# Causal attention in 32-row groups and units of four heads, instead of 96-row groups and units of two

## The reference, cut to what matters

```python
scores = jnp.einsum('bhqd,bhkd->bhqk', q, k) / jnp.sqrt(jnp.float32(HD))
causal = jnp.tril(jnp.ones((S, S), dtype=bool))
scores = jnp.where(causal[None, None], scores, jnp.finfo(scores.dtype).min)
attn = jax.nn.softmax(scores, axis=-1)
out = jnp.einsum('bhqk,bhkd->bhqd', attn, v)
out = out.transpose(0, 2, 1, 3).reshape(B, S, NQ * HD)
return out @ w_out
```

## Time and profile before

| | |
|---|---|
| median of three runs | 1374.59 us (1372.58 to 1374.79) |
| profiled execution, from the first to the last instruction (span) | 1397.1 us; what it took in all is not shown |
| TensorE (PE) busy | 1113.2 us, 80% of the span |
| VectorE (DVE) busy | 586.6 us, 42% |
| ScalarE (ACT) busy | 394.9 us, 28% |
| GpSimd (POOL) busy | 85.7 us, 6% |
| mean granted clock of TensorE | 0.871 of 2.4 GHz |

### The profile page before, as it was taken

The page is one execution under the profiler, slowest core; times in us unless marked ns, Lnnn a source line. Parts: engine busy times, 40 slices in busy tenths (PEclk is TensorE's granted clock), DMA queues, the critical chain, the costliest instruction groups (busy, mean ns, idle before and its releaser), DMA issues. The chain is left out here.

```text
span 1397.1 us, 24200 instructions
## 1 busy us (share of the span) xinstructions
PE 1113.2 (80%) x8646; PEld 771.9 (55%) x8647; DVE 586.6 (42%) x1737; ACT 394.9 (28%) x939; POOL 85.7 (6%) x128
## 2 busy tenths in 40 slices
PE   1999999998988889797793299955878978369992
PEld 0676677656565566555472177732645654247771
DVE  5272144224343465567486022215752672512222
ACT  2223312221414444343240133312421431013220
POOL 2000000000000000000000400022000000040003
PEclk9999988599999888898795599986979989579996
DMA  9100000000000000291003211118300000021113
GB/s 245 45 3 3 0 2 3 1 1 2 2 2 2 1 1 1 47 238 55 0 1 71 82 43 49 47 44 200 104 1 0 1 1 1 23 74 46 50 43 99
DMA packets 32137, 57.09 MB, mean 41 GB/s; under 512 B 3558, under 2 KB 28871, under 8 KB 31019
## 3 DMA queue, kind: packets, MB, share of 16 engines
q1 hardware_dynamic: 28856, 48.47, 12.8%
q0 software_dynamic: 3072, 6.30, 1.5%
q10 hardware_dynamic: 114, 1.04, 0.3%
HBM read 41.83 MB, written 13.86 MB: 40 GB/s over the span
## 5 line engine op out<-in xcount | busy, mean ns | idle before, releaser
L1932 PE MATMUL banks<-gu,sxT 96*128 x496 | 178.8, 505 | 0.8 <-ACT sxT L1967 0.4
L215 PE MATMUL banks<-xT,weights 96*96 96x512 f32 (+3 forms) x288 | 149.1, 668 | 1.2 <-ACT xT L616 0.9
L1333 ACT ACTIVATE work<-banks,nmax 128x128 f32<-128x128 f32 (+1 forms) x288 | 105.7, 418 | 108.0 <-DVE nmax L1372 107.7
L1993 DVE TENSOR_TENSOR h<-sg,banks 128x384 f32<-128x384 f32 x62 | 34.4, 555 | 237.7 <-ACT sg L1975 227.3
L1932 PEld LDWEIGHTS banks<-gu,sxT 96*128 96x128 f32 x496 | 93.1, 198 | 54.9 <-issue 8.1
L1372 DVE TENSOR_REDUCE nmax<-banks 128x2 f32<-128x256 f32 (+1 forms) x144 | 80.2, 557 | 64.7 <-PE banks L1277 62.4
L1252 PE MATMUL banks<-K,Q 96*128 96x128 f32 (+1 forms) x384 | 86.1, 351 | 11.1 <-PEq L88 11.1
L215 PEld LDWEIGHTS banks<-xT,weights 96*96 96x96 f32 (+3 forms) x288 | 53.5, 193 | 74.8 <-issue 67.3
L555 PE MATMUL banks<-Q,K 64*98 64x196 f32 (+2 forms) x960 | 78.7, 305 | 9.1 <-ACT work L688 9.1
L688 ACT ACTIVATE work<-banks 98x1024 f32<-98x1024 f32 (+1 forms) x48 | 49.2, 1025 | 114.7 <-PE banks L555 114.7
L555 PEld LDWEIGHTS banks<-Q,K 64*98 64x98 f32 (+1 forms) x960 | 67.2, 184 | 24.2 <-issue 22.5
(11 more groups left out here) (253 smaller groups left out, 1663.2 us busy)
## 6 DMA issues: line engine op xcount, KB each, us to landing
gu<-in_L2f_gu SPq DMA_DIRECT2D x1, 6912.0 KB, 36.7
xin<-slots_in SPq DMA_DIRECT2D x62, 96.0 KB, 1.9
slots_out<-y SPq DMA_DIRECT2D x62, 96.0 KB
gu<-in_L3f_gu SPq DMA_DIRECT2D x1, 5184.0 KB, 28.5
dn<-in_L2f_dn SPq DMA_DIRECT2D x1, 4608.0 KB, 47.6
slots_in<-zeros SPq DMA_DIRECT2D x1, 2976.0 KB, 22.5
dn<-in_L3f_dn SPq DMA_DIRECT2D x1, 2592.0 KB, 34.3
gu<-in_L2f_gu SPq DMA_DIRECT2D x1, 2304.0 KB, 13.1
```

The lines of the kernel that those rows point to most:

```text
L215: ins = nc.tensor.matmul(out, lhs(k, rows), rhs(k, rows), start=(k == 0), stop=(k == 1))
L1333: ins = nc.scalar.activation(w.Pr[0:rows, s % 3, hh, 0:lay.width(t)], S(s)[0:rows, hh, 0:lay.width(t)], ACT.Exp, bias=w.nmax[0:rows, s % 4 ...
L1932: ins = nc.tensor.matmul(banks[:, 2 + 2 * par + n, 0:EF], w.sxT[:, par, k, :], w.gu[:, bass.ds(e, 1), k, n * EF:(n + 1) * EF].rearrange("p ...
```

## The change

A unit is now four heads of one tile (12 units per stage instead of 24), and a head's scores contract 32 rows instead of 96: the two heads that share 32 rows are told apart by queries in which the other head's 16 rows are zero. So the queries are written in 4 copies (two chunks, even and odd heads) instead of 12, all by ScalarE with rope, two each by ScalarE and VectorE without. The scores of a unit fill two banks (`b`), and neighbours in issue order lie in different 32-row groups and different banks. There are two such pairs of banks, so unit s waits for the exponents of unit s-2. The mask is written first, and the scores are added to it. The turned exponents of a unit fill one bank (t = 0) or two halves in two banks (t = 1), which the next unit uses again; the outputs have one bank instead of two. In step s TensorE issues masks and scores of unit s, transposes of s-2 and values of s-3. VectorE takes one maximum per unit (four heads), copies one or two full banks, and issues a small step after each of these and one or two at the end of the step. The loop has 20 steps instead of 34. In L2f queries and keys lie in the space of the last 2 experts, so that 14 are loaded early and 2 late; the scratch of the rope lies in the work buffer.

```diff
+        def S(u):
+            return banks[:, 2 * (u % 2):2 * (u % 2) + 2, :].rearrange("p b (e k) -> p b e k", e=2)
+        def halves(u):
+            return 2 if place(u)[1] else 1
+        def turned_bank(half):
+            return banks[:, 4 + half, :]
+        O = banks[:, 6, 0:3 * P].rearrange("p (g q) -> p g q", q=P)
         @block.tensor
+            for s in range(N + 8):
+                if s < N:
+                    m, t, k = place(s)
+                    if s >= 2:
+                        pe.wait_ge(exp_ready, s - 1)
+                    for b in range(2):
+                        nc.tensor.matmul(S(s)[:, b, :, t * P:(t + 1) * P], env.ident16[:, :], env.mask16[:, :, :],
+                                         start=True, stop=False, skip_group_check=True)
+                    for e in range(2):
+                        for b in range(2):
+                            c, r = divmod(2 * k + b, 3)
+                            rows = slice(32 * r, 32 * r + 32)
+                            q0 = m * TOKENS + t * P
+                            ins = nc.tensor.matmul(S(s)[:, b, e, 0:(t + 1) * P], w.Q[rows, 2 * c + e, q0:q0 + P],
+                                                   w.K[rows, c, m * TOKENS:m * TOKENS + (t + 1) * P],
+                                                   start=False, stop=True, skip_group_check=True)
+                    ins.then_inc(scores_ready, 1)
+                u = s - 2
+                if 0 <= u < N:
+                    t = place(u)[1]
+                    pe.wait_ge(exp_ready, u + 1)
+                    for half in range(halves(u)):
+                        if u >= 1 and half < halves(u - 1):
+                            pe.wait_ge(copied, halves_before(u - 1) + half + 1)
+                        for i in range(4):
+                            j, chunk = (2 * half + i // 2, i % 2) if t else (i, 0)
+                            ins = nc.tensor.transpose(turned_bank(half)[:, i * P:(i + 1) * P],
+                                                      w.Pr[:, u % 3, j, chunk * P:(chunk + 1) * P], ident[:, :])
+                        ins.then_inc(turned, 1)
+                u = s - 3
+                if 0 <= u < N:
+                    m, t, k = place(u)
+                    pe.wait_ge(copied, halves_before(u + 1))
+                    if k == 0 and u >= UNITS:
+                        pe.wait_ge(O_out, u // UNITS)
...
         @block.vector
+            for s in range(N + 8):
+                if s < N:
+                    t = place(s)[1]
                     dve.wait_ge(scores_ready, s + 1)
                     if s >= 4:
                         dve.wait_ge(exp_ready, s - 3)
+                    nc.vector.tensor_reduce(w.nmax[:, s % 4, :].rearrange("p (b e) -> p b e", e=2), S(s)[:, :, :, 0:(t + 1) * P],
+                                            AX.X, ALU.max, negate=True).then_inc(max_ready, 1)
+                    between(1)
...
+                u = s - 2
+                if 0 <= u < N:
+                    for half in range(halves(u)):
+                        dve.wait_ge(turned, halves_before(u) + half + 1)
+                        if u >= 2 and half == 0:
+                            dve.wait_ge(pv_done, u - 1)
+                        nc.vector.tensor_copy(w.PT[:, u % 2, 2 * half:2 * half + 2, :, :].rearrange("p j c q -> p (j c q)"),
+                                              turned_bank(half)).then_inc(copied, 1)
+                        between(1)
...
+                between(2 if more_steps and s >= 6 else 1)
@@ causal_project
-    act_heads = [(c, j) for c in range(2) for j in range(6) if (j >= 2 if rope else c == 0)]
+    act_halves = [(c, e) for c in range(2) for e in range(2) if rope or c == 0]
@@ expert_buffers
-    early = x.stored if x.shared else n - 4
+    x.early = early = x.stored if x.shared else n - 2
@@ _constants
-    c["own"] = np.kron(np.eye(CH // HD), np.full((HD, 1), QSCALE)).astype(np.float32)
+    c["own"] = np.kron(np.tile(np.eye(2), (3, 1)), np.full((HD, 1), QSCALE)).astype(np.float32)
```

More of the change, by code:

```diff
@@ L1139, in _ @@
             dve.wait_ge(L1.added, 4)
[L1142 to L1198, removed]
@@ L1201, in attend @@
-def attend(nc, env, w, kind, ip, inner, into_x, behind_eps=None, behind_centre=False):
-    R, banks, ident = env.R, env.banks, env.ident
[L1208 to L1212, removed]
+UNITS = 3
+def attend(nc, env, w, ip, inner, into_x, behind_eps=None, more_steps=False):
+    R, banks, ident = env.R, env.banks, env.ident
+    tiles = [(m, t) for m in range(PAIR) for t in range(2)]
+    N = UNITS * len(tiles)
@@ L1218, in attend, with place @@
         projected, added, steps = sem("projected"), sem("added"), sem("steps")
[L1220 to L1225, removed]
+        def place(u):
+            tile, k = divmod(u, UNITS)
+            return (*tiles[tile], k)
         def S(u):
-            return banks[:, u % 3, :].rearrange("p (h k) -> p h k", h=2)
@@ new lines, in turned_bank, with tile_at, image_at @@
+        def turned_bank(half):
+            return banks[:, 4 + half, :]
+        O = banks[:, 6, 0:3 * P].rearrange("p (g q) -> p g q", q=P)
+        OM = banks[:, 7, 0:3 * P].rearrange("p (h d) -> p h d", d=32)
+        def tile_at(s, lag):
+            tile, k = divmod(s - lag, UNITS)
+            return tile if k == UNITS - 1 and 0 <= tile < len(tiles) else None
+        def image_at(s, lag):
+            tile = tile_at(s, lag)
+            return tile // 2 if tile is not None and tile % 2 == 1 else None
@@ L1292, in _ @@
                 if tile is not None:
-                    m, t, _ = units[s - 6]
-                    rows = lay.rows(t)
                     pe.wait_ge(O_out, tile + 1)
@@ L1363, in _, with between @@
             behind = None
-            both = kind == "causal" and behind_eps is not None
-            for s in range(U + 10):
-                if s < U:
-                    _, t, _ = units[s]
-                    rows = lay.rows(t)
+            def between(n):
+                for _ in range(n):
+                    if next(ahead, "done") == "done" and behind is not None:
+                        next(behind, None)
+            for s in range(N + 8):
+                if s < N:
+                    t = place(s)[1]
                     dve.wait_ge(scores_ready, s + 1)
```

189 lines of the change are left out of this document (59 added, 130 removed).

## The result

The changed kernel is 1.5% slower: 1394.38 us (median of 4 runs, 1387.54 to 1396.95) against 1373.63 for the kernel before, ratio 1.0151 [1.0118, 1.0184]. Its profiled execution took 1392.7 us, span 1390.9. The forecast was 1345, range 1325 to 1368. Times in this document are medians of all runs of a kernel, while ratios leave out runs that took over 1.5% longer than the fastest of their kernel.

A forecast was written before the change was run, and what follows sets the result against it. TensorE bounds the attention stages, VectorE after the change. Fill 7.1, steps 22.85, drain 4.4 and 6.5 make 40.9 us; six stages plus 3 and 3.2 are 251.6 against 281.67, so 1345 us, range 1325 to 1368.

The forecast's parts named there:

- the clock in the fill: Start of each attention stage: TensorE at half speed, clock rising during step 2; 7.1 us to the maximum of s=3.
- the clock falls: Rival, chance 0.03: TensorE's waits inside every step bring the clock to 1.2 GHz, over 100 us later, about 1450.
- The changes of shape: TensorE's steps: four changes per four heads instead of two, 0.09 us each; with drains of 0.16, 3 us over six stages.
- Overlap of the row groups: Scores in neighbouring 32-row groups run side by side: four heads 0.87 us for 256 keys, 0.45 for 128.
- Nine steps s = 3 to 11: Middle of each attention stage, VectorE's steps of 1.8 to 3.2 us summing to 22.85 us, TensorE's a little under.
- The prediction's own prices for TensorE: A four-head step takes TensorE 2.8 us against 3.5 for 256 keys, 1.7 against 2.0 for 128.
- VectorE's prices: VectorE in attention steps: maximum over 1024 columns 1.23 us busy, 1.14 in a row; one-bank copy 0.60; small steps 0.19.
- the better case: Chance 0.08: small steps fill VectorE's waits, half of 6.7 us per stage gained; 1325 us.
- Copies and transposes: Rival, chance 0.16: with one bank per half, transposes and copies wait for each other, 3.6 us per stage; 1366.
- Fill and drain: Attention stage ends: fill 7.1 us, 4.4 after s=11 until the last value matmuls, then 6.5 to the last addition.
- The rest at nothing: Outside the attention stages: fewer query copies, later key rotation and moved expert loads are hidden, changing the time by 0.
- The span against the runs: Profiled span 1397.1 us, 1.6% above the runs' median 1374.59, no view says where; saving of 30 scaled to 29.5.

The follow-up runs named there:

- w3: Changed kernel plus 20 mask matmuls at the end of each projection and the masks of step 1 issued six times; 1341.94 us, ratio 0.9759 against before.
- m3: Kernel before plus a tiny matmul (two instructions of 8 columns) over 64 rows ahead of each unit's scores; 1551.89 us, ratio 1.1263.
- m4: Changed order with 96-row scores, plus a tiny 32-row matmul ahead of each four-head unit's masks; 1408.84 us, ratio 1.0226 against before.
- n1: Changed order with 96-row scores, half of the score matmuls left out (output differs); 1340.78 us, ratio 0.9728 against before.
- e1: Changed kernel, but each head's scores contract 96 rows again, from 12 query copies; 1376.33 us, ratio 0.9978 against before.
- m1: Kernel before plus a tiny matmul (two instructions of 8 columns) over 32 rows ahead of each unit's scores; 1557.20 us, ratio 1.1318.
- m2: Kernel before plus a tiny matmul (two instructions of 8 columns) over 96 rows ahead of each unit's scores; 1480.52 us, ratio 1.0774.
- e4: Changed kernel plus 20 mask matmuls at the end of each projection; 1388.51 us, ratio 1.0081 against before.
- h_four_then_32_tail: Changed order, scores over 96 rows in steps 0 to 3 and 32 after, plus 20 mask matmuls ending each projection; 1342.73 us, ratio 0.9760 against before.

## Why the prediction was wrong

**The step that failed** is the clock in the fill. The prediction let the clock rise during step 2 ("clock in between") and gave "1 us more" to three stages. Measured, step 7 of the first stage begins 24.49 us after the stage's first matmul in the changed kernel (460.27 to 484.76) and 15.49 in w3 (459.41 to 474.90), 9.0 us apart. In the six stages this is 7.4 to 9.4 us, 51.5 together, of the 53.8 us between 300.11 and 246.29. These 53.8 are the loss against before (19.25) and the 34.6 by which the stages of w3 are shorter than before's 280.86.

**The rival "the clock falls"** was the right one, with a chance of 0.03. Its argument against, the full clock of the earlier trace rows, compared a stage that already ran at full speed with one that starts at half; m3 shows the same 64 rows at 0.50 for most of a stage once they interrupt these steps. Its price (1450) took half speed for all nine steps; it ends after the first half of a stage. Its cause was also another: not waits in every step, but a low clock at the start that the new sequence does not raise (TensorE busy 23.65 of 23.93), and, from a warm start, one wait between 32-row steps. Which property of the sequence keeps it low stays open in part: changes of grouping give some of it (m4), less work per step alone does not (n1).

**The changes of shape** were priced at a gap of 0.09 each, with a drain of 3 us over six stages named beside the sum and not in it. Directly they cost just the gap: from the two masks to the scores 0.32 in w3 (464.47 to 464.79) against 0.23 in e1 with its 96 rows (470.65 to 470.88). What they do to the clock was not priced, although the text noted that no row of before has this sequence.

What w3 shows of the other steps, at a full clock:

- **Overlap of the row groups**: right. Eight scores of 32 x 256 are followed after 1.06 us (forecast 0.97 with the gap), of 32 x 128 after 0.65 (0.55). In e1, without overlap, such scores take 1.73 (465.20 to 466.93) and 0.90 (463.11 to 464.01).
- **Nine steps s = 3 to 11**: 23.34 us against 22.85. That the number fits is luck, for TensorE bounds them, not VectorE. The prediction's own prices for TensorE add up to some 20.4 us over these steps; the transposes of the outputs were left out (0.38 from 474.52 to 474.90), and scores and transposes took 1.06 and 0.59 where the prices with a gap are 0.96 and 0.52:

```profile
464.47:487.81 23.34, 23.30 (x248) 15.28 (x248) 21.08 (x59) 13.61 (x40) 0.00 (x0) 1.00 0.01 2
```

- **VectorE's prices** held (a maximum over 1024 columns 1.22 busy). Small steps filled its waits, which the better case had foreseen; the gain of that case did not come, as TensorE was the bound. Copies and transposes do not take turns: the page of w3 has no idle time of TensorE ahead of the transposes.

```profile
L1222 PE MATMUL banks<-small,work 128*128 128x128 f32 x432 | 62.7, 281 | 0.0
```

- **Fill and drain**: 5.40 us from step 11's end to the last values (forecast 4.4) and 6.74 from there to the end (6.5). The stages sum to 246.29 us against the forecast 251.6, with a warmer start than was assumed and 10 masks more.
- **The rest at nothing**: 3.4 us more outside the stages, within what two profiles differ by.
- **The span against the runs**: that "no view says where" the 1.6% lay was an omission; the windows view names the stretch at 0.53. It did not move the forecast, which scaled by the ratio.

## What to carry to other kernels

Before costing a change of TensorE's instruction mix, look at the granted clock where the stage starts, and price the new sequence at both levels: a mix can hold a full clock and yet be unable to raise a low one. Where that is so, a few matmuls that keep TensorE going up to the stage and through the first wait of its pipeline can be worth more than the saving itself (here 52 us from 1394.38 to 1341.94, against a forecast saving of 29.5). A busy share near 1 at a clock of 0.5 is no sign of a well-fed engine: look for short matmuls and changes of row grouping inside it.

## What was not expected of the hardware

- Two instructions of 8 columns per unit, 144 tiny matmuls added to a kernel of 1374 us, made it 13% slower (m1) and 7.7% without a change of grouping (m2). By themselves, at full speed, they would be some 46 us (144 x 0.32, the price in m4) and at most 30 (144 x 0.21, 489.64 to 489.85 in m2); the stages grew by 175.7 and 93.1.
- The two levels have a memory here: the same steps 0 to 6 of 32-row scores ran at 0.51 in the first half of the changed kernel's stage and at full speed in w3 (459.41 to 484.00 at 1.00), with nothing different but 20 masks ahead and ten in step 1.
- A single wait of 1.00 us between 32-row steps is followed by about 20 us at half speed (e4). One of 0.41 us one step later is not (w3), nor is one of 0.84 us at the same place between 96-row steps (h_four_then_32_tail).
